# Tile 6 finished between the halves of tile 7's right product, and the gates of tiles 2 to 5 computed in pairs

## The chip, the cores and the metric

The kernel runs on one core of a Trainium2 chip. The metric is the device time of one launch in microseconds (us). The core's engines are TensorE (PE, matrix products), VectorE (DVE), ScalarE (ACT), GpSimd (POOL) and SyncE (SP, which here only issues transfers). Each takes its own instructions strictly in the order in which they are written and waits on semaphores for the others.

## The reference, cut to what matters

For eight tiles x(t) of 128 tokens by 512 features, each with its own adapter number:

```
y = x W + (x A[i]) B[i]                      # base product and the tile's low-rank adapter, rank 16
logits = y W_gate^T                          # 8 experts
p = softmax(logits); keep the top 2, divide by their sum  -> route_w
h = y A_e^T for each expert e (8 x 16 columns);  hw = h * route_w
out = x + y W_base^T + b + hw B              # B: 128 x 512
```

The input is float32 throughout, and the top 2 must come out right.

## The kernel before, in words

The weights are folded first: W is multiplied once with the gate, the experts' A and W_base, and the identity is added, so that a tile needs only x times the folded matrix (648 columns), a low-rank correction, and `hw B`. Precision is kept by splitting each operand into a high part in fp32r and the remainder (`hi`, `lo`); `product` (L808) then issues three matmuls. A split is a cast by ScalarE and a subtraction by VectorE (`lo`, L588).

A tile's result lies in two banks of PSUM. The **left** bank holds the logits (8 columns), h (128 columns) and half of the output, the **right** bank the other half. `Left` and `Right` are its products (tiles 0 to 3). Tiles 4 to 7 are computed two at a time, pair q = 2 with tiles 4 and 5 and pair q = 3 with tiles 6 and 7, by Strassen's scheme with seven products instead of eight, `M1` to `M7`: M5, M4, M3 and M2 fill the left banks; M1, M7 and M6 go into the right ones, with sums in between on VectorE (`sum_e`, `sum_z`, `seed_u`, `sum_u1`, `sum_u2`). Pair 2 has its sums written into the bank ahead of M7 and M6 (`seed_u`); pair 3 has them added at the end (L802, L805).

For a pair q of tiles, `T1(q)` transposes x A, ScalarE copies it (`copy_xa_t`), and `Lora_left(q)` and `Lora_right` multiply it with the adapter part. With `Lora_left(q)` the logits of both tiles are complete, and the gate runs on VectorE (`gate(t)`, L729): max of 8, difference to the first (`top_diff`), index, one-hot, then after ScalarE's `exp_top(t)` the weights and `hw`. `T2(t)` transposes hw, ScalarE and VectorE split the result (`split_hw(t)` on each, through one bank, so that tile t+1's T2 waits for tile t's split), and `Delta(t)` multiplies it with `ffn_b` into the left bank and then the right one (for tile 7 right, then left). ScalarE copies the banks to the output tile (`copy_left`, `copy_right`), which frees them for tile t+4 (left) and t+2 (right): M5(3) waits for the third copy_left, M4(3) for the fourth (L865, L873).

Nothing plans the order: it is written out by hand, one list for each engine. TensorE's list is L1028 to L1080, ScalarE's L526 to L583, VectorE's L751 to L805, GpSimd's L393 to L403 (it forms the sums of x and the low-rank parts, and is done at 38 us), and SyncE's ends with the output transfers, tile by tile (L316 to L325). The left half of tile 7 is sent by ScalarE itself (L583). Since the lists are in order, a wait in one holds up all that stands behind it. The splits that stand between the gates in VectorE's and ScalarE's lists (`split_x_outer`, `split_x_inner`, `split_xd`, `split_cs`) serve the products of pairs 2 and 3.

Of the kernel before, what the change touches and what calls it, by code (L numbers as in the profile page):

```python
# [42 lines left out]
def adaln_ffn_kernel(nc, x_t, itok, fold_in, lora, ffn_b, bias, out):  # L43
    ctx = ExitStack()
    with ctx:
# [161 lines left out]
        def left(t):  # L207
            return left_bank[t % 4]
# [118 lines left out]
        def gpsimd_program(pool):  # L327
# [64 lines left out]

            pool.wait_ge(lora_loaded, NT * DMA)  # L393
# [9 lines left out]
            split_la_pair(3)  # L403

        def scalar_program(act):
# [135 lines left out]
            exp_top(2)  # L541
            copy_right(0)
            copy_right(1)
            exp_top(3)
# [3 lines left out]
            split_cs(SUM7, 4)  # L548
            copy_right_a(2)
# [7 lines left out]
            split_cs(SUM6, 1)  # L557
            copy_left(2)
            exp_top(4)
# [3 lines left out]
            exp_top(5)  # L563
# [12 lines left out]
            copy_left(5)  # L576
            copy_right(5)
            split_hw(6)
            split_hw(7)
# [5 lines left out]
        def vector_program(dve):  # L585
# [111 lines left out]
            def sum_u2(q):  # L697
                k = SEVEN.index(q)
                dve.wait_ge(u1_done, k + 1)
                dve.wait_ge(z_done, k + 1)  # L700
                nc.vector.tensor_tensor(mix(q)[:, 2], mix(q)[:, 2], mix(q)[:, 0], ALU.add).then_inc(u2_done, 1)

# [47 lines left out]

            dve.wait_ge(const_ready, 4)  # L751
# [17 lines left out]
            gate(2)  # L769
            gate(3)  # L770
            sum_e(2)
            split_xa(4)
# [8 lines left out]
            gate(4)  # L781
            gate(5)
            split_hw(4)
            seed_u(2)
            split_cs(SUM7, 2)
            sum_e(3)
            split_xa(6)
            split_cs(SUM6, 3)
# [10 lines left out]
            sum_u2(3)  # L799

            dve.wait_ge(zr_done, NT - 1)
# [5 lines left out]
        def tensor_program(pe):  # L807
# [81 lines left out]
            def seven_right(out, q, which, done, seeded):  # L889
# [3 lines left out]
                for c in range(2):  # L893
                    mm = product(out, xd_chunk(x_hi, q, which, c), xd_chunk(x_lo, q, which, c),
                                 cs_hi[:, which, c, :], cs_lo[:, which, c, :], c == 0 and not seeded, False)
# [11 lines left out]
            def M6(q):  # L907
                pe.wait_ge(yr_done, 2 * q)
                seven_right(right(2 * q + 1), q, SUM6, 3, q == SEVEN[0])
# [135 lines left out]
            M4(2)  # L1045
            T2(2)
            M3(2)
            M2(2)
            T2(3)

            Right(2, ALL)
            T1(2)
# [6 lines left out]
            M4(3)  # L1059
            T2(4)  # L1060
            M1(2)
            M3(3)
            M2(3)
            T2(5)

            M7(2)
            T1(3)
            M6(2)
# [4 lines left out]
            Delta(5)  # L1073
            M7(3)
            T2(6)
            M6(3)
            Lora_right(3, (6, 7))
            T2(7)
            Delta(6)
            Delta(7)  # L1080
# [42 lines left out]
```

## Time and profile before

| | us |
|---|---|
| median of 3 runs | 66.23 (65.94 to 67.05) |
| profiled execution, time | 66.37 |
| its span, first to last instruction | 65.2 |
| TensorE busy | 60.0 (92%), 406 matmuls |
| VectorE busy | 49.9 (77%), 155 instructions |
| ScalarE busy | 33.9 (52%), 91 instructions |
| GpSimd busy | 22.9 (35%), 45 instructions |
| last output transfers, issue to landing | 2.2 (SyncE, 128 KB), 2.9 (ScalarE, 128 KB) |

A row of a timeline tells when an instruction (or a run of like ones) started, how long it took, its engine, its line, the operation and shapes, and in brackets how long the engine had been idle before it and who released it. Instructions overlap in the engines' pipelines, so the next may start before the duration of the one ahead is over; what counts for a queue is the spacing of the starts. Helpers have one line for all calls (a product's matmuls are L809 to L811, every subtraction of a split is L589), so an instruction is told by its tiles and its place in the list. The transposes T1 and T2 are L921 and L952, Lora_left is L935, Lora_right L942.

### The profile page before, as it was taken

How to read it: one execution, taken by the hardware profiler on the slowest of the kernel's cores; microseconds unless marked ns; L12 is line 12 of the kernel's file. 1: busy time of each engine (PE TensorE's matmuls, PEld its weight loads, DVE VectorE, ACT ScalarE, POOL GpSimd, SP SyncE). 2: the span in 40 equal slices, each digit the busy share in tenths (PEclk: the TensorE clock that was granted, in tenths of full speed). 3: DMA queues.
4: the chain of work that ended last, by engine and by line, in shares of the span. 5: the costliest groups of instructions: out<-in, count | busy, mean ns of one | idle time of the engine just before them, and what ended most of it. 6: DMA issues, size and time to landing. Idle time of an engine off the chain costs nothing.

```text
span 65.2 us, 1329 instructions
## 1 busy us (share of the span) xinstructions
PE 60.0 (92%) x406; PEld 58.3 (89%) x406; DVE 49.9 (77%) x155; ACT 33.9 (52%) x91; POOL 22.9 (35%) x45
## 2 busy tenths in 40 slices
PE   4989999999999999999999997999999999999900
PEld 4969999999999999999998995999999997999600
DVE  0957999908799999998888568669766699886800
ACT  2753999315799394452170955478084713452310
POOL 1000799899404994994059930000000000000000
PEclk9999999999999999999999999999999999999999
DMA  0799999404994035323233330810008000034072
GB/s 0 223 339 376 381 398 401 154 3 126 358 329 169 6 96 129 67 61 70 57 78 64 67 79 18 293 49 0 0 9 313 10 0 0 0 134 175 13 263 64
DMA packets 5529, 8.75 MB, mean 134 GB/s; under 512 B 1009, under 2 KB 2065, under 8 KB 5522
## 3 DMA queue, kind: packets, MB, share of 16 engines
q1 hardware_dynamic: 4978, 7.88, 37.4%
q0 software_dynamic: 256, 0.52, 2.3%
q10 hardware_dynamic: 288, 0.27, 1.2%
q8 instruction: 3, 0.05, 0.3%
q14 instruction: 4, 0.03, 0.1%
HBM read 5.26 MB, written 2.10 MB: 113 GB/s over the span
## 4 chain that ended last, share of the span: by engine, by line
PE 78%; DVE 7%; DMA 5%; issue 2%; ACT 2%; DVEq 0%; ACTq 0%
PE bank L809 19%; PE bank L811 18%; PE bank L810 18%; PE bank L817 8%; PE bank L819 5%; DMA w_raw<-fold_in 5%; PE bank L983 3%; PE bank L935 2%; DVE cs_lo L589 2%; PE bank L942 1%; PE bank L987 1%; PE bank L952 1%; PE bank L921 1%; DVE top_diff L735 1%; DVE bank L685 1%
## 5 line engine op out<-in xcount | busy, mean ns | idle before, releaser
L809 PE MATMUL bank<-c_hi,x_hi 128*128 128x408 f32 (+1 forms) x40 | 13.6, 339 | 0.5 <-ACT x_raw L516 0.5
L811 PE MATMUL bank<-c_hi,x_lo 128*128 128x408 f32 (+1 forms) x40 | 13.4, 335 | 0.0
L810 PE MATMUL bank<-c_lo,x_hi 128*128 128x408 f32 (+1 forms) x40 | 13.4, 334 | 0.0
L809 PEld LDWEIGHTS bank<-c_hi,x_hi 128*128 128x128 f32 x40 | 7.5, 188 | 0.8 <-issue 0.8
L589 DVE TENSOR_TENSOR x_lo<-x_raw,x_hi 128x512 fp32r<-128x512 f32 (+1 forms) x10 | 8.0, 824 | 0.0
L810 PEld LDWEIGHTS bank<-c_lo,x_hi 128*128 128x128 f32 x40 | 7.5, 188 | 0.0
L811 PEld LDWEIGHTS bank<-c_hi,x_lo 128*128 128x128 f32 x40 | 7.5, 188 | 0.0
L331 POOL DMA_DIRECT2D lora_raw<-lora x8 | 4.4, 554 | 6.5 <-issue 6.3
L496 ACT ACTIVATE top_exp<-top_diff 128x2 f32<-128x2 f32 x8 | 1.6, 204 | 6.8 <-DVE top_diff L735 6.8
L809 PE MATMUL bank<-ffn_b_hi,hw_hi 128*128 128x256 f32 x16 | 4.9, 305 | 0.0
L811 PE MATMUL bank<-ffn_b_hi,hw_lo 128*128 128x256 f32 x16 | 4.5, 282 | 0.0
L810 PE MATMUL bank<-ffn_b_lo,hw_hi 128*128 128x256 f32 x16 | 4.5, 282 | 0.0
L507 ACT COPY w_raw<-bank 128x256 f32<-128x256 f32 x8 | 2.9, 373 | 2.6 <-PE bank L811 2.5
L503 ACT CAST hw_hi<-bank 128x128 fp32r<-128x128 f32 x8 | 2.1, 267 | 3.3 <-PE bank L952 3.3
L809 PE MATMUL bank<-cs_hi,x_hi 128*128 128x256 f32 x12 | 3.7, 310 | 0.0
L411 ACT CAST wt_hi<-w_raw 128x512 fp32r<-128x512 f32 x4 | 2.5, 620 | 2.3 <-DMA w_raw<-fold_in 2.1
L589 DVE TENSOR_TENSOR hw_lo<-bank,hw_hi 128x128 fp32r<-128x128 f32 x8 | 2.3, 288 | 1.7 <-ACT hw_hi L503 1.7
L977 PE MATMUL bank<-const-bfloat16-1.0 128*128 128x128 bf16 x24 | 2.7, 309 | 0.9 <-PEq L1116 0.9
L589 DVE TENSOR_TENSOR wg_lo<-w_raw,wg_hi 128x648 fp32r<-128x648 f32 (+2 forms) x5 | 3.4, 696 | 0.1
L810 PE MATMUL bank<-cs_lo,x_hi 128*128 128x256 f32 x12 | 3.4, 282 | 0.0
L811 PE MATMUL bank<-cs_hi,x_lo 128*128 128x256 f32 x12 | 3.4, 281 | 0.0
L586 DVE MEMSET bw_rows<- 128x2592 f32 x1 | 2.2, 2218 | 1.5 <-PEq L1116 1.5
(140 smaller groups left out, 188.7 us busy)
## 6 DMA issues: line engine op xcount, KB each, us to landing
x_raw<-x_t SPq DMA_DIRECT2D x8, 256.0 KB, 4.2
out<-w_raw SPq DMA_DIRECT2D x7, 256.0 KB, 2.2
w_raw<-fold_in SPq DMA_DIRECT2D x4, 256.0 KB, 4.6
w_raw<-fold_in SPq DMA_DIRECT2D x3, 324.0 KB, 4.6
bw_rows<-bw_hi SPq DMA_DIRECT2D x16, 40.5 KB, 2.1
lora_raw<-lora POOLq DMA_DIRECT2D x8, 64.0 KB, 3.3
bw_rows<-bw_lo SPq DMA_DIRECT2D x8, 40.5 KB, 2.1
ffn_b_raw<-ffn_b SPq DMA_DIRECT2D x1, 256.0 KB, 5.7
```

Of the source, the lines that this page charges most:

```text
L331: pool.dma_start(lora_raw[:, b, :], lora[bass.ds(adapters[b], 1), :, :].rearrange("a p c -> (a p) c")).then_inc(lora_loaded, DMA)
L411: nc.scalar.copy(wt_hi[:, m, :], raw_wt(m)).then_inc(w_hi_done, 1)
L503: nc.scalar.copy(hw_hi[:, t % 2, :], t2_bank[:, 0:P]).then_inc(hw_hi_done, 1)
L507: nc.scalar.copy(y_out[:, t, y_of_left_bank(t)], left(t)[:, in_left_bank(t)]).then_inc(yl_done, 1)
L586: nc.vector.memset(bw_rows[:, 0].bitcast(F32), 0.0).then_inc(even_zeros, 1)
L589: nc.vector.tensor_tensor(out, raw, hi.bitcast(F32), ALU.subtract).then_inc(done, 1)
L809: nc.tensor.matmul(out, a_hi, b_hi, start=first, stop=False, skip_group_check=True)
L810: nc.tensor.matmul(out, a_hi, b_lo, start=False, stop=False, skip_group_check=True)
L811: return nc.tensor.matmul(out, a_lo, b_hi, start=False, stop=last, skip_group_check=True)
L817: nc.tensor.matmul(bank[i][:, cols], w[:, m, rows], wg[:, m, cols], start=False, stop=False, skip_group_check=True)
L819: nc.tensor.matmul(fold_right(i), w[:, m, rows], wg[:, m, LEFT:], start=False, stop=False, skip_group_check=True)
L977: nc.tensor.matmul(bwr_bank[:, 0:P], ones, ones, start=True, stop=True)
```

## The change

TensorE's list: T2(2) goes behind M3(2), T2(3) behind Right(2), T2(4) behind M1(2), T2(5) behind M7(2), T2(6) ahead of M7(3). M6(3) is cut into its two chunks; between them stand the Lora_right of tile 6, T2(7) and Delta(6), and behind the second chunk the Lora_right of tile 7 and Delta(7).

VectorE's list: gates 2 and 3, and gates 4 and 5, become `gate_pair`, which takes each step for both tiles, with one instruction where the shapes allow it (top_diff, one-hot, reciprocal, weights, route) and two where they don't (max, index, hw). Gates 0, 1, 6 and 7 are as they were. split_cs(SUM7) goes ahead of split_xa(4), split_cs(SUM6) ahead of the hw split of tile 4. sum_u2(3) leaves VectorE for GpSimd, where it waits for the gate of tile 7 as well.

ScalarE's list: exp_top(3) goes ahead of copy_right(0), exp_top(4) and (5) ahead of copy_left(2), split_cs(SUM6) to just behind split_cs(SUM7), and copy_left(5) behind split_hw(6).

No matmul is added or left out.

```diff
--- before.py
+++ after.py
@@ -390,6 +390,13 @@
                                         ALU.subtract).then_inc(la_lo_done, 1)
                 pool.wait_ge(la_lo_done, b + 1)
 
+            def sum_u2(q):
+                k = SEVEN.index(q)
+                pool.wait_ge(z_done, k + 1)
+                pool.wait_ge(hw_done, 2 * q + 2)
+                pool.wait_ge(u1_done, k + 1)
+                nc.gpsimd.tensor_tensor(mix(q)[:, 2], mix(q)[:, 2], mix(q)[:, 0], ALU.add).then_inc(u2_done, 1)
+
             pool.wait_ge(lora_loaded, NT * DMA)
             split_la(0)
             split_la(1)
@@ -401,6 +408,7 @@
             split_la_pair(2)
             sum_x_inner(3)
             split_la_pair(3)
+            sum_u2(3)
 
         def scalar_program(act):
             act.dma_start(w_raw[:, 0, FIRST:D + GH], fold_in[0, :, FIRST:D + GH]).then_inc(w_first_loaded, DMA)
@@ -539,13 +547,14 @@
             copy_left(0)
             copy_left(1)
             exp_top(2)
+            exp_top(3)
             copy_right(0)
             copy_right(1)
-            exp_top(3)
             copy_m5(2)
             copy_m4(2)
             split_hw(2)
             split_cs(SUM7, 4)
+            split_cs(SUM6, 1)
             copy_right_a(2)
             split_hw(3)
             act.wait_ge(x_loaded[6], DMA)
@@ -554,13 +563,12 @@
             split_x_inner(3)
 
             copy_xa_t(2)
-            split_cs(SUM6, 1)
+            exp_top(4)
+            exp_top(5)
             copy_left(2)
-            exp_top(4)
             copy_right(2)
             copy_left(3)
             copy_right(3)
-            exp_top(5)
             copy_m5(3)
             copy_m4(3)
             split_hw(4)
@@ -573,9 +581,9 @@
             copy_left(4)
             copy_right(4)
             exp_top(7)
-            copy_left(5)
             copy_right(5)
             split_hw(6)
+            copy_left(5)
             split_hw(7)
             copy_left(6)
             copy_left(7)
@@ -694,12 +702,6 @@
                 dve.wait_ge(m1_done, k + 1)
                 nc.vector.tensor_tensor(mix(q)[:, 0], first_bank[:, M1_COLS], mix(q)[:, 0], ALU.add).then_inc(u1_done, 1)
 
-            def sum_u2(q):
-                k = SEVEN.index(q)
-                dve.wait_ge(u1_done, k + 1)
-                dve.wait_ge(z_done, k + 1)
-                nc.vector.tensor_tensor(mix(q)[:, 2], mix(q)[:, 2], mix(q)[:, 0], ALU.add).then_inc(u2_done, 1)
-
             steps = [0]
 
             def step(instruction):
@@ -748,6 +750,34 @@
                                                scalar=top_rcp[:, n], in1=route[:, n].unsqueeze(2).broadcast_to([P, E, R]),
                                                op0=ALU.mult, op1=ALU.mult).then_inc(hw_done, 1)
 
+            def gate_pair(q):
+
+                pair = (2 * q, 2 * q + 1)
+                dve.wait_ge(lg_done, q + 1)
+                for t in pair:
+                    top = nc.vector.max(top_val[:, t % 2], left(t)[:, gate_cols(t)])
+                step(top)
+                nc.vector.tensor_tensor(top_diff[:], top_val[:, :, 0:TOP], top_val[:, :, 0:1].broadcast_to([P, 2, TOP]),
+                                        ALU.subtract).then_inc(diff_done, 2)
+                for t in pair:
+                    top = nc.vector.max_index(top_idx[:, t % 2], top_val[:, t % 2], left(t)[:, gate_cols(t)])
+                step(top)
+                step(nc.vector.tensor_tensor(onehot[:], expert_id[:].unsqueeze(1).unsqueeze(1).broadcast_to([P, 2, TOP, E]),
+                                             top_idx[:, :, 0:TOP].unsqueeze(3).broadcast_to([P, 2, TOP, E]), ALU.is_equal))
+                dve.wait_ge(exp_done, pair[1] + 1)
+                nc.vector.reciprocal(top_rcp[:], top_sum[:])
+                step(nc.vector.tensor_tensor(weighted[:], onehot[:],
+                                             top_exp[:].unsqueeze(3).broadcast_to([P, 2, TOP, E]), ALU.mult))
+                step(nc.vector.tensor_tensor(route[:], weighted[:, :, 0, :], weighted[:, :, 1, :], ALU.add))
+                for t in pair:
+                    n = t % 2
+                    if t >= 2:
+                        dve.wait_ge(t2_done, t - 1)
+                    h = left(t)[:, h_cols(t)].rearrange("p (e r) -> p e r", e=E)
+                    nc.vector.scalar_tensor_tensor(out=hw[:, n].rearrange("p (e r) -> p e r", e=E), in0=h,
+                                                   scalar=top_rcp[:, n], in1=route[:, n].unsqueeze(2).broadcast_to([P, E, R]),
+                                                   op0=ALU.mult, op1=ALU.mult).then_inc(hw_done, 1)
+
             dve.wait_ge(const_ready, 4)
             split_xa(0)
             split_xa(1)
@@ -766,9 +796,9 @@
             split_hw(1)
             split_cs(SUM1, 1)
 
-            gate(2)
-            gate(3)
+            gate_pair(1)
             sum_e(2)
+            split_cs(SUM7, 2)
             split_xa(4)
             split_hw(2)
             split_xa(5)
@@ -778,14 +808,12 @@
             split_x_inner(3)
             split_xd(2)
 
-            gate(4)
-            gate(5)
+            gate_pair(2)
+            split_cs(SUM6, 3)
             split_hw(4)
             seed_u(2)
-            split_cs(SUM7, 2)
             sum_e(3)
             split_xa(6)
-            split_cs(SUM6, 3)
             split_xa(7)
             split_hw(5)
             sum_z(3)
@@ -796,8 +824,8 @@
             split_hw(6)
             sum_u1(3)
             split_hw(7)
-            sum_u2(3)
-
+
+            dve.wait_ge(u1_done, len(SEVEN))
             dve.wait_ge(zr_done, NT - 1)
             nc.vector.tensor_tensor(y_out[:, NT - 2, 0:HALF], right(NT - 2), mix(3)[:, 0], ALU.add).then_inc(last_right_done, 1)
             dve.wait_ge(u2_done, len(SEVEN))
@@ -886,11 +914,11 @@
                 pe.wait_ge(m4_copied, SEVEN.index(q) + 1)
                 seven_left(2 * q + 1, 0, C01, q, False).then_inc(left_done, 1)
 
-            def seven_right(out, q, which, done, seeded):
+            def seven_right(out, q, which, done, seeded, chunks=(0, 1)):
                 pe.wait_ge(xd_lo_done, SEVEN.index(q) + 1)
                 if q == SEVEN[0]:
                     pe.wait_ge(cs_lo_done, done)
-                for c in range(2):
+                for c in chunks:
                     mm = product(out, xd_chunk(x_hi, q, which, c), xd_chunk(x_lo, q, which, c),
                                  cs_hi[:, which, c, :], cs_lo[:, which, c, :], c == 0 and not seeded, False)
                 return mm
@@ -904,9 +932,9 @@
                 pe.wait_ge(yr_done, 2 * q - 1)
                 seven_right(right(2 * q), q, SUM7, 2, q == SEVEN[0])
 
-            def M6(q):
+            def M6(q, chunks):
                 pe.wait_ge(yr_done, 2 * q)
-                seven_right(right(2 * q + 1), q, SUM6, 3, q == SEVEN[0])
+                seven_right(right(2 * q + 1), q, SUM6, 3, q == SEVEN[0], chunks)
 
             def T1(q):
                 pe.wait_ge(xa_done, 2 * q + 2)
@@ -1043,12 +1071,12 @@
             Lora_left(1)
             M5(2)
             M4(2)
+            M3(2)
             T2(2)
-            M3(2)
             M2(2)
+
+            Right(2, ALL)
             T2(3)
-
-            Right(2, ALL)
             T1(2)
             Right(3, ALL)
             Lora_left(2)
@@ -1057,26 +1085,28 @@
             Delta(3)
             M5(3)
             M4(3)
+            M1(2)
             T2(4)
-            M1(2)
             M3(3)
             M2(3)
+
+            M7(2)
             T2(5)
-
-            M7(2)
             T1(3)
-            M6(2)
+            M6(2, (0, 1))
             Lora_left(3)
             Lora_right(2, (4, 5))
             Delta(4)
             M1(3)
             Delta(5)
+            T2(6)
             M7(3)
-            T2(6)
-            M6(3)
-            Lora_right(3, (6, 7))
+            M6(3, (0,))
+            Lora_right(3, (6,))
             T2(7)
             Delta(6)
+            M6(3, (1,))
+            Lora_right(3, (7,))
             Delta(7)
 
         sync_program(nc.sync)
```

## Rows read from the trace of the kernel before

**Rows 1.** Windows view: stretch, length, busy us (instructions) per engine, clock, DMA, GB/s.

```profile
36.00:66.00 30.00, 25.19 (x176) 24.11 (x174) 20.06 (x86) 13.47 (x48) 2.07 (x6) 1.00 0.24 80
```

**Rows 2.** TensorE timeline: start us, duration us, engine, line, operation [idle before <- releaser].

```profile
39.66 0.35 PE L811 MATMUL bank<-c_hi,x_lo 128*128 128x408 f32 x1
39.84 0.27 PE L952 MATMUL bank<-ident,hw 128*128 128x128 f32 x1
40.59 0.43 PE L809 MATMUL bank<-c_hi,x_hi 128*128 128x408 f32 x1 [0.47 <-ACT x_raw L516]
```

**Rows 3.** ScalarE timeline around exp_top(2), the right copies, exp_top(3), copy of M5.

```profile
38.29 0.20 ACT L496 ACTIVATE top_exp<-top_diff 128x2 f32<-128x2 f32 x1 [0.79 <-DVE top_diff L735]
...
38.49 0.62 ACT L511 COPY w_raw<-bank 128x256 f32<-128x256 f32 x2
39.89 0.20 ACT L496 ACTIVATE top_exp<-top_diff 128x2 f32<-128x2 f32 x1 [0.77 <-DVE top_diff L735]
...
40.09 0.35 ACT L516 COPY x_raw<-bank 128x256 f32<-128x256 f32 x1
```

**Rows 4.** VectorE timeline: tile 2's gate, then tile 3's top_diff.

```profile
38.02 0.23 DVE L735 TENSOR_SCALAR top_diff<-top_val 128x2 f32<-128x2 f32 x1
...
38.69 0.16 DVE L741 RECIPROCAL top_rcp<-top_sum 128x1 f32<-128x1 f32 x1
38.77 0.16 DVE L742 TENSOR_TENSOR weighted<-onehot,top_exp 128x16 f32<-128x16 f32 x1
...
39.63 0.23 DVE L735 TENSOR_SCALAR top_diff<-top_val 128x2 f32<-128x2 f32 x1
```

**Rows 5.** TensorE timeline: T2(3), T1(2), Lora_left(2), M5(3).

```profile
42.90 0.27 PE L952 MATMUL bank<-ident,hw 128*128 128x128 f32 x1
...
44.43 0.27 PE L921 MATMUL bank<-ident,xa_rows 128*114 128x128 f32 x1
...
45.96 0.52 PE L935 MATMUL bank<-bw_rows,xa_t 114*128 114x392 f32 x2
...
47.99 0.35 PE L809 MATMUL bank<-c_hi,x_hi 128*128 128x408 f32 x1
```

**Rows 6.** VectorE timeline: hw split of tile 3, sum_z(2), wide splits, gate(4).

```profile
43.51 0.29 DVE L589 TENSOR_TENSOR hw_lo<-bank,hw_hi 128x128 fp32r<-128x128 f32 x1
43.72 0.41 DVE L672 TENSOR_TENSOR x_raw<-x_raw,bank 128x256 f32<-128x256 f32 x1
44.04 2.16 DVE L589 TENSOR_TENSOR x_lo<-x_raw,x_hi 128x512 fp32r<-128x512 f32 x3
46.52 0.17 DVE L734 MAX8 top_val<-bank 128x8 f32<-128x8 f32 x1 [0.32 <-PE bank L935]
```

**Rows 7.** ScalarE timeline: hw split of tile 3, copy of T1(2), copy_left(2).

```profile
43.21 0.27 ACT L503 CAST hw_hi<-bank 128x128 fp32r<-128x128 f32 x1 [0.42 <-PE bank L952]
...
44.73 0.27 ACT L492 CAST xa_t<-bank 114x128 fp32r<-114x128 f32 x1 [0.22 <-PE bank L921]
...
47.11 0.37 ACT L507 COPY w_raw<-bank 128x256 f32<-128x256 f32 x1 [1.59 <-PE bank L811]
```

**Rows 8.** TensorE and VectorE timelines: T2(5), Lora_left(3); split_xd(3).

```profile
53.28 0.27 PE L952 MATMUL bank<-ident,hw 128*128 128x128 f32 x1
...
55.28 0.52 PE L935 MATMUL bank<-bw_rows,xa_t 114*128 114x392 f32 x2
...
54.80 0.95 DVE L589 TENSOR_TENSOR x_lo<-x_raw,x_hi 128x768 fp32r<-128x768 f32 x1
```

**Rows 9.** TensorE and ScalarE timelines: last matmul of Delta(6), first of Delta(7), last copy.

```profile
60.57 0.28 PE L811 MATMUL bank<-ffn_b_hi,hw_lo 128*128 128x256 f32 x1
60.82 0.39 PE L809 MATMUL bank<-ffn_b_hi,hw_hi 128*128 128x256 f32 x1
...
61.84 0.37 ACT L507 COPY w_raw<-bank 128x256 f32<-128x256 f32 x1 [0.93 <-PE bank L811]
```

**Rows 10.** GpSimd timeline: the sum of 512 columns, nearest to the sum moved there.

```profile
23.12 1.30 POOL L370 TENSOR_TENSOR x_raw<-x_raw 128x512 f32<-128x512 f32 x1
```

## The prediction

> **What bounds the kernel now.** First the busy time by engine over the second half. From 36 us to the end of the instructions TensorE (PE) is busy 25.2 of 30.0 us, and the last 3.5 us of these hold only the last copy and its transfer; its granted clock is 1.00 [rows 1]. So the set work of TensorE is the spine, and a change that adds and removes no matmul can move the end only through the gaps between matmuls and through what stands behind the last one. The timeline then shows these gaps. The large one is at M3(2): the transpose before it starts at 39.84, the first matmul of M3(2) at 40.59 with 0.47 us idle before it, released by the copy of M5 on ScalarE [rows 2]. That copy (40.09) stood in ScalarE's queue behind exp_top(3), which started at 39.89 [rows 3], because its input, tile 3's top_diff, was written only at 39.63, 1.61 us after tile 2's, by the serial gates on VectorE [rows 4]. The two others are small. From T2(5) at 53.28 to Lora_left(3) at 55.28 [rows 8] lie twelve matmuls (1.43 by the spacing worked out below) and two transposes (0.2), which leaves 0.3: T1(3) waits there for VectorE. And Delta(7) starts at 60.82, 0.25 behind its neighbour instead of 0.12 [rows 9]. With 0.7 for the first (below) the gaps are worth about 1.1 us, which is the most that this change can give.
>
> **Part 1: gates of tiles 2 and 3 as a pair, both exps ahead of the right copies.** The pair has one top_diff write for both tiles. What precedes it is one max more. The trace shows unwaited neighbours on VectorE 0.08 us apart (38.69 to 38.77), and waited ones about 0.20 (the eight steps of a gate take 1.61, 38.02 to 39.63) [rows 4]; the second max is unwaited, so I take 0.08 and keep 0.20 as the upper end. Top_diff of both then starts at 38.10 instead of 38.02 and 39.63. ScalarE followed top_diff by 0.27 (38.02 to 38.29) and an exp held it 0.20 [rows 3, 4]: exps at 38.37 and 38.57, the two right copies (0.62 together) from 38.77, the copy of M5 at 39.39 instead of 40.09. A copy started 0.50 before the matmul that waits for it (40.09 to 40.59) [rows 2, 3], so M3(2) can start at 39.89. TensorE reaches it at 39.84, since T2(2) now stands behind it. Gain at M3(2): 0.7 us. T2(2) used to lie in the stall and now costs its own time. Its price alone isn't in the rows; between 0.06 (by its 128 columns, from the spacings 0.12 for 256 [rows 9] and 0.18 for 408 [rows 2]) and 0.27, I take 0.1. Net: TensorE is 0.6 us ahead from M2(2) on. If the second max took 0.20, it would be 0.5.
>
> A page's rule speaks against the pair. The rows show the 0.08 us between two unwaited instructions [rows 4]. The Trainium skill, VectorE: DVE Perf Modes, section The DRAIN you can't avoid, says that the pipeline empties after every operation and that leaving out the semaphore between operations saves nothing. By that rule the second max, find and scaling would cost full steps, the pair's top_diff would be 0.12 us later twice, and the sum below would come out 0.1 to 0.2 us higher; the row decides, and I stay with 0.08.
>
> **Part 2: T2(3) behind Right(2).** This is where I expect the gain to be given back. Before, T2(3) started at 42.90; twelve matmuls of Right(2) lie between it and T1(2) at 44.43, so they take 1.43 us, 0.119 each [rows 5]. After, T2(3) starts at 42.90 - 0.6 + 1.43 = 43.73, 0.83 later than before although TensorE is ahead. ScalarE split tile 3's hw at 43.21, 0.31 behind the transpose, VectorE at 43.51, another 0.30 [rows 5 to 7]. So VectorE's split_hw(3) comes at 44.34, and queued behind it on VectorE are sum_z(2) and three splits of 512 and more columns (2.16 us together): from 43.51 to 46.20 now [rows 6], 2.69 us, hence to 47.03 after. VectorE had only 0.32 us idle ahead of gate(4) at 46.52 [rows 6], so 0.83 of delay comes through as 0.5: the pair of tiles 4 and 5 starts at 47.03. On ScalarE the two splits of x and the copy of T1(2)'s result stand behind split_hw(3) as well. They ended 0.22 before T1(2) let the copy go at 44.73 [rows 7]; 0.83 later they put that copy at 45.3, and Lora_left(2), which TensorE would reach at 45.96 - 0.6 = 45.36 [rows 5], starts at about 45.6 (0.27 of copy and 0.05 behind it). That takes 0.2 of the gain. VectorE's split_cs(SUM7), moved ahead of split_xa(4), waits for ScalarE's split of the same tile behind split_hw(2) at about 42.1 and runs 0.6 us; split_xa(5) is then done at about 43.7, just when T1(2) wants it. I cost it at nothing; the cover has no slack, so the upper end is 0.3. In its old place it stood 0.6 us ahead of split_xa(6) and (7), as SUM6's did, and T1(3) waited for these: its gap of 0.3 goes.
>
> **Part 3: exps of tiles 4 and 5 ahead of copy_left(2).** Before, copy_left(2) started at 47.11, ahead of exp_top(4) [rows 7], and M5(3) at 47.99 without a wait [rows 5]. M5(3) overwrites the bank that this copy empties. Now the copy stands behind both exps, and they behind the pair's top_diff: 47.03 + 0.21 + 0.08 = 47.32 for top_diff (0.21 is one waited step), exps at 47.6 and 47.8, the copy at 48.0, M5(3) at 48.5 by the 0.50 above. TensorE gets there at 45.6 + (47.99 - 45.96) = 47.63 [rows 5]. New stall: 0.9 us. M5(3) is at 48.5 against 47.99: TensorE has gone from 0.6 ahead to 0.5 behind. M4(3) finds its bank empty: copy_left(3) follows by 0.5, M4(3) by 1.1. This term hangs on VectorE's 0.83 of delay: were the pair there at 46.1, when Lora_left(2) ends, the copy would stand at 47.1 and the stall would be nil. Between those ends (0 and 0.9, 1.1 with slow pair steps) I take 0.9, since each link has its row.
>
> **Part 4: T2(5) behind M7(2).** T2(5) was at 53.28 [rows 8]; after it is at 53.28 + 0.5 + 6 x 0.119 = 54.5. ScalarE +0.31, VectorE +0.30, sum_z(3) +0.21 (43.51 to 43.72) [rows 6]: 55.35. Lora_left(3) waits for sum_z(3), which takes 0.41: 55.35 + 0.41 + 0.1 = 55.85, against 55.28 before. TensorE alone would be there at 55.28 + 0.5 - 0.3 = 55.5: a wait of 0.35. VectorE goes on with split_xd(3) (0.95 [rows 8]) from 55.7 and starts gate(6) at 56.65.
>
> **Part 5: the end.** Gates 6 and 7 stay serial, 1.61 us each [rows 4]: done at 59.85. Then split_hw(6), 0.29 and 0.05 behind it: T2(7) at 60.2 (it needs that bank free). TensorE would be there at 59.9: from Lora_left(3) two matmuls at 0.18, thirty at 0.119 and T2(6), 4.0 us. That is 0.3 of wait. Behind it come Delta(6) (6 matmuls), the second half of M6 (3) and one Lora_right (1): 10 x 0.119 + 0.1 = 1.3, and a restart after a wait costs some 0.07. Delta(7) starts at 61.55. It was at 60.82 [rows 9]: +0.73, with the 0.13 in it that the new order wins by hiding tile 7's hw split, so that Delta(7) no longer waits. Last copy 61.84 + 0.7 = 62.5 [rows 9], the transfer behind it as before. Sum_u2(3) on GpSimd: 256 columns took VectorE 0.41, and the nearest GpSimd row is 1.30 for 512 columns [rows 10], so 0.65 to 1.30. It starts at about 60.6 (behind sum_u1(3) and gate 7) and is done at 61.9 at worst; VectorE's last add needs it at 62.2. Hidden, worth nothing; VectorE loses 0.33 of work where it waits for TensorE anyway. Output transfers on SyncE keep their order; tile 6's leaves more ahead of the last ones, which can give 0 to 0.3 (I take 0).
>
> **Sum**, against the profiled execution (66.37 us, span 65.2): -0.7 (M3) + 0.1 (T2) + 0.2 (Lora_left(2)) + 0.9 (M5(3)) - 0.3 (T1(3)) + 0.35 (Lora_left(3)) + 0.3 (T2(7)) - 0.13 (Delta(7)) = +0.7, so 67.07. That execution stands 0.14 above the median of the three runs (66.23), so the median to expect is 66.95.
>
> **Rivals.**
> (a) Forecast, new waits at Lora_left(2), M5(3) and Lora_left(3): +0.7 (own range +0.3 to +1.2), chance 0.75. For it: each link is an in-order queue with a row, and the 0.32 us of slack on VectorE is smaller than the 0.83 of delay.
> (b) Not slower: the pair of tiles 4 and 5 comes in time, as VectorE makes up for the late T2(3) or its wide splits run faster behind a late start. Then M5(3) starts at 47.6 and the end comes 0.2 earlier than now (66.0); with sum_z(3) in time as well, 0.7 to 0.8 earlier (65.45). It decides from the point where VectorE is free at 46.2 instead of 47.03. Chance 0.18. Against it: nothing on VectorE between split_hw(3) and the pair is taken out.
> (c) Slower by over 2%: the clock. TensorE now idles 0.9 us at M5(3), longer than in any gap named above. In the rows the granted clock stays 1.00 across the 0.47 us gap [rows 1, 2]; no row shows it at the lower level here. If it fell to half after 48.5, each 0.7 us of matmuls would cost 0.7 more, and with one such stretch the time is 67.65. Chance 0.05.
> (d) The change doesn't do what it says: the copy of M5 still comes late (ScalarE waits for the second exp), so the first gain is missing: +1.2 to +1.4, 67.5. Chance 0.02, as both exps need just one top_diff.
>
> **The numbers.** Point 66.95, from (a). Two per cent, about what a measurement of this kernel can tell from no change, is 1.32 us: 64.9 and 67.55. The three runs shown spread by 1.1 us, so a median carries 0.2 to 0.3 of its own. Faster by over 2% needs (b) whole and a low median: 0.03. Slower by over 2%: (c), (d) and the upper end of (a): 0.09. Within: 0.88. Range 66.15 to 67.6: it leaves out most of (b) and some of the upper ends, about 2 in 10.
>
> **What would show it.** In the changed kernel's timeline: no idle ahead of M3(2) (right: start near 39.9); T2(3) near 43.7, VectorE's next gate near 47.0; TensorE idle ahead of M5(3) by 0.8 to 0.9 us, released by a copy to the output on ScalarE; a short wait at Lora_left(3) for the subtraction on VectorE; no idle ahead of Delta(7). Wrong would be: M5(3) without a wait, or the granted clock below 1.00, or the last transfer released by VectorE's add.

## The result, and the profile after

The change makes the kernel about 1% faster: median 65.68 us against 66.41 in 21 runs each, ratio 0.990 (95% interval 0.987 to 0.9925), so 0.7 us. I had forecast 66.95, 0.7 us slower than the 66.23 I knew, with a range from 66.15. The sign is wrong, and that the size is the same is chance: the trace says in which part I was wrong. The ratio compares the fast executions of both kernels alone; each kernel has some that take about 1 us longer, and they count in the medians.

The profiled executions themselves differ in a part that the change doesn't touch. That of the changed kernel took 66.56 us, more than the 66.37 before. Up to M4(2) both lists of TensorE are the same; Lora_left(1), two products ahead of that point, starts at 37.25 us before and at 38.11 after, and between 36.75 and 38.11 in the profiled executions of all kernels below. So I count stages from it (times "from Lora_left(1)"), and let only the timed runs say what a kernel is worth as a whole.

TensorE's timeline of the changed kernel, from the Lora_left of pair 1 on: Lora_left(1) itself, the first matmul of M3(2), T2(3), Lora_left(2), M5(3), T2(5), Lora_left(3), T2(7), tile 7's Lora_right, and Delta(7).

```profile
38.11 0.52 PE L963 MATMUL bank<-bw_rows,xa_t 114*128 114x392 f32 x2
...
40.71 0.35 PE L837 MATMUL bank<-c_hi,x_hi 128*128 128x408 f32 x1
...
44.46 0.27 PE L980 MATMUL bank<-ident,hw 128*128 128x128 f32 x1
...
46.30 0.64 PE L963 MATMUL bank<-bw_rows,xa_t 114*128 114x392 f32 x2
...
49.11 0.42 PE L837 MATMUL bank<-c_hi,x_hi 128*128 128x408 f32 x1 [0.51 <-ACT w_raw L515]
...
55.19 0.27 PE L980 MATMUL bank<-ident,hw 128*128 128x128 f32 x1
...
56.56 0.59 PE L963 MATMUL bank<-bw_rows,xa_t 114*128 114x392 f32 x2 [0.28 <-DVE x_raw L680]
...
60.83 0.30 PE L980 MATMUL bank<-ident,hw 128*128 128x128 f32 x1
...
62.03 0.28 PE L970 MATMUL bank<-bw_rows,xa_t 114*128 114x256 f32 x1
62.15 0.28 PE L837 MATMUL bank<-ffn_b_hi,hw_hi 128*128 128x256 f32 x1
```

The last two rows show Delta(7) start 0.12 us behind the matmul ahead of it, without a wait, where it waited before [rows 9]. The idle ahead of M3(2) [rows 2] is gone. In its place stand the two waits that I had named, at M5(3) for a copy to the output on ScalarE and at Lora_left(3) for the subtraction `sum_z(3)` on VectorE (L680).

VectorE and ScalarE in the same kernel, the rows that answer to [rows 6] and [rows 7]: the hw split of tile 3, sum_z(2), the three wide splits and the gate pair of tiles 4 and 5; on ScalarE that tile's cast, the two exps and copy_left(2).

```profile
45.07 0.29 DVE L597 TENSOR_TENSOR hw_lo<-bank,hw_hi 128x128 fp32r<-128x128 f32 x1 [0.62 <-ACT hw_hi L511]
45.28 0.41 DVE L680 TENSOR_TENSOR x_raw<-x_raw,bank 128x256 f32<-128x256 f32 x1
45.61 2.16 DVE L597 TENSOR_TENSOR x_lo<-x_raw,x_hi 128x512 fp32r<-128x512 f32 x3
47.68 0.24 DVE L758 MAX8 top_val<-bank 128x8 f32<-128x8 f32 x2
48.03 0.16 DVE L760 TENSOR_TENSOR top_diff<-top_val 128x4 f32<-128x4 f32 x1
```

```profile
44.77 0.27 ACT L511 CAST hw_hi<-bank 128x128 fp32r<-128x128 f32 x1 [0.42 <-PE bank L980]
...
48.23 0.20 ACT L504 ACTIVATE top_exp<-top_diff 128x2 f32<-128x2 f32 x1 [1.98 <-DVE top_diff L760]
...
48.43 0.19 ACT L504 ACTIVATE top_exp<-top_diff 128x2 f32<-128x2 f32 x1
...
48.62 0.35 ACT L515 COPY w_raw<-bank 128x256 f32<-128x256 f32 x1
```

VectorE's wide splits end at 47.77 and the gate pair starts without idle, so ScalarE stands idle for 1.98 us ahead of the exp, with copy_left(2) behind it, whose matmuls were done at 47.5.

| from Lora_left(1), us | before | forecast | after |
|---|---|---|---|
| M3(2) | 3.34 | 2.64 | 2.60 |
| T2(3) | 5.65 | 6.48 | 6.35 |
| Lora_left(2) | 8.71 | 8.35 | 8.19 |
| M5(3) | 10.74 | 11.25 | 11.00 |
| Lora_left(3) | 18.03 | 18.60 | 18.45 |
| Delta(7) | 23.57 | 24.30 | 24.04 |
| last copy on ScalarE | 24.59 | 25.25 | 24.95 |
| end of span behind the last copy's start | 3.34 | as before | 2.31 |

Up to the last copy the changed kernel is 0.36 us **slower**. It wins 1.03 us behind it, where I had put 0 (0.3 at most). The two make -0.67, which is what the timed runs give. The 0.36 is no accident of one trace: two more kernels with the changed kernel's body, padded ones below, have their last copy at 24.94 and 25.01, and one with the body of before, the one without tile 6's transfer, has it at 24.55. The view of transfers shows where the rest lies: first rows for the changed kernel from 63 us to its end (mean busy share of the 16 transfer engines in tenths, GB/s, and by issue the size and the time to landing), and then for the kernel before from 63 us to its end (the q14 row gives packets, MB and share of a queue).

```profile
DMA  0000549998998997415999999999997300000000
GB/s 0 0 0 0 205 171 444 444 410 307 375 444 307 410 410 273 137 51 171 307 358 375 358 358 325 342 342 324 358 358 239 120 17 0 0 0 0 0 0 0
...
out<-w_raw ACTq DMA_DIRECT2D x1, 128.0 KB, 1.9
```

```profile
GB/s 373 335 317 466 354 372 317 280 280 373 372 317 354 317 168 75 19 0 19 0 37 19 19 37 19 19 19 37 19 19 19 0 0 0 0 0 0 0 0 0
...
q14 instruction: 1, 0.01, 0.9%
```

Each number of a GB/s line is one fortieth of the window, here 0.055 to 0.06 us. In the changed kernel the last bytes flow at 307 to 375 GB/s until they run out. Before, they flow at 280 to 466 GB/s for 0.8 us and then at 0 to 37, some 20 in the mean, for another 0.8 us: about a sixteenth of the rate, as if one of the 16 transfer engines were finishing its share alone. The same view from 63.93 to 64.73 us, the slow rest by itself, has the two output queues and nothing else:

```profile
DMA packets 17, 0.02 MB, mean 19 GB/s; under 512 B 2, under 2 KB 17, under 8 KB 17
...
q10 hardware_dynamic: 9, 0.01, 2.9%
q1 hardware_dynamic: 8, 0.01, 2.8%
```

The packets' times in the trace, which the view only sums up, have these 17 one behind the other, with 5 ns of overlap at most: seven of 1 KB of SyncE's transfer (q1), then eight of 1 KB of ScalarE's (q10), each group followed by one packet of 4 bytes, and most of them 0.042 us apart. From 63 us on there is one packet of a kind that the changed kernel's end doesn't have: 8 KB (0.01 MB) on the instruction queue q14, from 63.20 to 63.51. The page of the kernel before counts four such fetches in the span, that of the changed kernel three.

```profile
q14 instruction: 4, 0.03, 0.1%
```

```profile
q14 instruction: 3, 0.02, 0.1%
```

Whether the order of the transfers or the fetch did it is what the experiments had to show.

### The profile page after: what moved, and what is told of

It reads as the page before. It is cut to its first block, busy times and chain, and to the rows that moved or that the text cites. A ratio compares the mean times of both kernels' runs of the same rounds, so it can differ in the third digit from the quotient of the medians.

```text
span 65.4 us, 1319 instructions
## 1 busy us (share of the span) xinstructions
PE 60.8 (93%) x406; PEld 59.0 (90%) x406; DVE 47.4 (72%) x144; ACT 33.8 (52%) x91; POOL 22.6 (34%) x46
## 4 chain that ended last, share of the span: by engine, by line
PE 82%; DVE 6%; DMA 5%; ACT 3%; issue 1%; DVEq 0%
PE bank L837 20%; PE bank L839 19%; PE bank L838 19%; PE bank L845 8%; PE bank L847 5%; DMA w_raw<-fold_in 5%; PE bank L1011 3%; DVE x_lo L597 3%; PE bank L963 2%; PE bank L980 2%; PE bank L1015 2%; PE bank L970 1%; DVE x_raw L680 1%; ACT w_raw L515 1%; DVE hw_lo L597 1%
## 5 line engine op out<-in xcount | busy, mean ns | idle before, releaser
L398 POOL TENSOR_TENSOR x_raw<-x_raw 128x256 f32<-128x256 f32 x1 | 0.7, 739 | 22.2 <-DVE x_raw L703 22.2
```

## The experiments

**The end alone, and all but the end.** My first theory (T) was that tile 6's 256 KB, now sent earlier relative to the last halves, no longer crowd them. The rival (B) was that the body gains.

```diff
 # the kernel before, with (lines of the list joined)
-            M7(3); T2(6); M6(3); Lora_right(3, (6, 7)); T2(7); Delta(6); Delta(7)
+            T2(6); M7(3); M6(3, (0,)); Lora_right(3, (6,)); T2(7); Delta(6); M6(3, (1,)); Lora_right(3, (7,)); Delta(7)
 # sum_u2(3) from VectorE to GpSimd, copy_left(5) behind split_hw(6)
```

> The kernel before with the end of the change alone: M6(3) in two halves with tile 6 finished between them, T2(6) ahead of M7(3), copy_left(5) behind split_hw(6), sum_u2(3) on GpSimd. Gates and the transposes of tiles 2 to 5 stay as before. Theory T (the gain lies in the transfers at the end: tile 6's 256 KB leave earlier relative to the last two halves of tile 7, so the last one lands in 1.9 us and not 2.9): 0.9 to 1.2 us faster than before, more than the whole change, with the last copy at most 0.2 earlier. Theory B (the gain lies in the body, the end is worth what my prediction gave it): 0 to 0.3 us faster.

Measured: ratio 0.998 (0.993 to 1.003), no difference; last copy 24.45 from Lora_left(1), 0.14 earlier than before, and ScalarE's transfer took 2.9 us again. T's 0.9 to 1.2 us isn't there; B's 0 to 0.3 isn't excluded (the interval is 0.5 faster to 0.2 slower).

```profile
DMA  0000004999999726999999971001001000000000
...
q14 instruction: 1, 0.01, 0.5%
...
out<-w_raw ACTq DMA_DIRECT2D x1, 128.0 KB, 2.9
```

Here tile 6's transfer is clearly apart from the last two (the dip to 2 in the line of the window 62 us to the end), and the slow rest is there all the same, with the instruction fetch (64.15 us).

```diff
 # the changed kernel, with the end put back as it was before
```

> The changed kernel with the end put back: M7(3), T2(6), M6(3) whole, Lora_right of both tiles, T2(7), Delta(6), Delta(7); copy_left(5) ahead of copy_right(5); sum_u2(3) on VectorE. Gates in pairs and the later transposes stay. Theory T: slower than before by 0.2 to 0.5 us, since M5(3) and Lora_left(3) wait (Lora_left(1) to last copy 0.3 to 0.5 longer) and the last transfer lands in 2.9 us as before. Theory B: faster by 0.4 to 0.7 us.

Measured: ratio 0.996 (0.992 to 1.000). The last copy comes at 25.05, 0.46 later than before, so by T this kernel should have been slower. It isn't (0.3 us faster, between 0 and 0.5), since its transfer landed in 2.0 us although the order of the last transfers is that of before, and there is no q14 row:

```profile
out<-w_raw SPq DMA_DIRECT2D x1, 256.0 KB, 2.0
out<-w_raw SPq DMA_DIRECT2D x1, 128.0 KB, 1.9
out<-w_raw ACTq DMA_DIRECT2D x1, 128.0 KB, 2.0
```

Theory T falls with these two, and B with them, since the body of this kernel is the slower one. The long landing comes with the fetch, and the fetch at the end is missing where the gates are in pairs.

A small part is left for T. In the three kernels with the old end and no fetch in it (this one, the padded kernel before and the one with the first pair alone) ScalarE's transfer lands in 2.04 us, and in the five with the new end and no fetch in it in 1.87 or 1.88. So of the 1.03 us behind the last copy, about 0.87 goes with the fetch and 0.16 with the new order.

**The last transfers with less beside them.**

```diff
 # the kernel before, with (the waits beside it left out)
-            for t in range(NT - 1):        # output transfers of SyncE
+            for t in range(NT - 2):
```

> The kernel before without the output transfer of tile 6 (its rows of the output are not written, and nothing waits for them); all computation is as before. Theory T: the two last transfers have the queues to themselves, the one issued by ScalarE lands in about 2.0 us instead of 2.9, and the time is 0.8 to 1.0 us less. Theory B: at most 0.2 us less.

Measured: ratio 0.990 (0.985 to 0.995), 0.7 us, between what T and B named; landing 2.4 us, fetch at the end present. With half the bytes in the queues the transfer still took longer than the 1.9 us of the changed kernel, which sends them all. By the packets, fifteen of the sixteen shares were through 1.49 us behind the issue (1.69 before), and the late one 0.42 behind them (0.79 before). So this kernel mixes less crowding, 0.2 us, with a milder meeting of fetch and output, and prices neither alone.

**The fetch, moved without touching any work.** Theory F: VectorE's program is read in blocks of 8 KB, and before the change a block boundary is reached while the last output is on its way; the paired gates shorten the program (the trace has 191 instructions of VectorE before, waits counted, and 178 after; 190 with the end alone, 179 without the end), and the boundary is no longer reached. If so, instructions that do nothing should be able to bring the gain and to take it away. `even_zeros` is a semaphore raised at about 3.7 us, so that waiting for it costs only the instruction; two waits share one, as 32 of them make 207 out of 191.

```diff
 # the kernel before, with VectorE's list at its start and ahead of gate(2)
+            for _ in range(16):
+                dve.wait_ge(even_zeros, 1)
```

> The kernel before with 16 waits for a raised semaphore at the start of VectorE's list and 16 ahead of gate(2), both where VectorE is idle: its program becomes longer, so that the boundary at which the last fetch falls is passed well before the end. Theory F: the fetch comes before 62 us, ScalarE's transfer lands in about 2.0 us, and the time is 0.5 to 1.0 us less than before, with no work taken out. Theory T, or a gain by fewer instructions as such: the same or slower by up to 0.3 us.

Measured: ratio 0.9905 (0.985 to 0.996), so as much as the change gained, with 16 instructions more and nothing taken out. The last copy came 0.11 later (24.70; 0.09 of it is there at M3(2), behind the waits ahead of gate(2)), the transfer landed in 2.0 us, and the fetch starts at 58.95 us, in the window from 58.5 to 59.5:

```profile
q14 instruction: 1, 0.01, 2.1%
```

and in the last 1.9 us (from 62 us on) there is none:

```profile
GB/s 172 474 345 345 517 302 388 259 517 259 474 259 474 302 345 345 324 345 366 366 366 302 324 345 324 345 345 345 345 281 173 65 0 0 0 0 0 0 0 0
...
out<-w_raw ACTq DMA_DIRECT2D x1, 128.0 KB, 2.0
```

The same waits in the kernel with the end alone price the new end with the fetch out of the way:

```diff
 # the kernel with the end alone, with the same 32 waits
```

> The kernel with the end of the change alone (tile 6 between the halves of tile 7's right product, sum_u2(3) on GpSimd), with the same 32 waits as in the padded kernel before. Against that kernel it prices the new end by itself with the fetch out of the way. Theory F: 0.1 to 0.2 us faster than the padded kernel before (0.7 to 1.1 faster than before). Theory T: 0.9 to 1.1 faster than the padded kernel before.

Measured: ratio 0.989 (0.983 to 0.996), against 0.9905 for the padded kernel before: the timed runs tell no difference. But this pair doesn't price the new end cleanly, since the moved fetch brings a pause on VectorE. Its row and that of T2(7) on TensorE:

```profile
58.27 0.16 DVE L745 RECIPROCAL top_rcp<-top_sum 128x1 f32<-128x1 f32 x1 [0.45 <-DVE onehot L742]
...
59.44 0.30 PE L958 MATMUL bank<-ident,hw 128*128 128x128 f32 x1 [0.36 <-DVE hw_lo L597]
```

From one-hot to reciprocal in gate 7 VectorE takes 0.62 us here and in the padded kernel before, and 0.25 in the kernel before. The late instruction is the 192nd of VectorE's trace in both padded kernels, and the fetch follows it by 0.65 to 0.67 us; the kernel before has only 191. So a block boundary seems to hold VectorE up as well, though only these two traces show it. The old end hides the pause; the new one needs tile 7's hw earlier, T2(7) waits, and the last copy comes at 24.91. Without padding it came at 24.45, 0.14 earlier than before. With the 0.16 of the landing the new end is worth some 0.3 us by the spans, where no pause meets it.

**The reverse, first in the wrong place.**

```diff
 # the changed kernel, behind VectorE's last addition
+            for _ in range(26):
+                dve.wait_ge(e_done, 1)
```

> The changed kernel with 26 waits for a semaphore that was long ago raised, at the very end of VectorE's list, behind its last addition: nothing waits for them, and VectorE's program gets the length that it had before the change. Theory F (the gain of the change is a fetch of 8 KB of instructions that fell into the last output transfers and no longer does, since the paired gates make VectorE's program shorter): an instruction fetch is back in the last 2 us of the trace, ScalarE's output transfer lands in 2.8 to 3.0 us instead of 1.9, and the time is 0.6 to 1.1 us above the changed kernel's (0 to 0.5 slower than before). Theory T (the order of the last transfers): no difference from the changed kernel, 0.7 faster than before.

Measured: ratio 0.990 (0.982 to 0.998), as the changed kernel. The fetch is back, as the window from 64.0 to the end at 64.4 shows, but it starts at 64.2, when the output's packets are through:

```profile
GB/s 0 0 0 0 0 0 0 0 0 0 0 0 0 0 0 0 0 0 0 819 0 0 0 0 0 0 0 0 0 0 0 0 0 0 0 0 0 0 0 0
DMA packets 1, 0.01 MB, mean 20 GB/s; under 512 B 0, under 2 KB 0, under 8 KB 0
...
q14 instruction: 1, 0.01, 8.2%
```

My expectation failed on that: a program of the old length isn't enough, the fetch has to meet the packets. The waits stood behind the last addition and ran until 63.05, and with them the point at which VectorE asks for the block came later. So the same 26 waits ahead of the hw split of tile 4, where VectorE idles for 2.2 us:

```diff
             split_cs(SUM6, 3)
+            for _ in range(26):
+                dve.wait_ge(even_zeros, 1)
             split_hw(4)
```

> The changed kernel with the same 26 waits for a raised semaphore as the kernel padded at its end, but ahead of the hw split of tile 4, where VectorE is idle for 2.2 us. VectorE's program has the old length, and its last instructions stand where they stood in it before the change. Theory F: VectorE's last fetch falls between 0.5 us before and 1.0 us behind the start of ScalarE's output packets, and that transfer lands in 2.4 to 3.0 us instead of 1.9; the time is 0.5 to 1.0 us above the changed kernel's, 0.2 faster to 0.4 slower than before. If the landing of 2.9 in the kernel before has another cause: as the changed kernel, 0.7 faster than before.

Measured: ratio 0.997 (0.993 to 1.001): two thirds of the change's gain gone (0.5 of 0.7 us; the intervals of the two kernels, 0.987 to 0.9925 and 0.993 to 1.001, only just stay apart). The last copy is where the changed kernel has it (24.94 from Lora_left(1), against 24.95), the transfer landed in 2.5 us, and the slow rest is back at 17 to 34 GB/s with the fetch in the window (63 us to the end):

```profile
GB/s 478 375 341 410 307 375 137 103 120 239 478 324 375 341 325 273 376 358 324 307 290 154 34 0 17 17 34 17 34 17 17 34 0 0 0 0 0 0 0 0
...
q14 instruction: 1, 0.01, 0.9%
...
out<-w_raw ACTq DMA_DIRECT2D x1, 128.0 KB, 2.5
```

**The waits that the change makes.**

```diff
 # the changed kernel, with
             copy_xa_t(2)
-            exp_top(4)
-            exp_top(5)
             copy_left(2)
             copy_right(2)
             copy_left(3)
             copy_right(3)
+            exp_top(4)
+            exp_top(5)
```

> The changed kernel with exp_top(4) and (5) behind the four output copies of tiles 2 and 3 instead of ahead of them. Theory T: the 0.5 us wait of TensorE at M5(3) goes, and the end comes 0.4 to 0.9 us earlier than the changed kernel's (1.1 to 1.6 earlier than before). Theory B, or if the waits behind M5(3) swallow it: as the changed kernel, within 0.1.

Measured: ratio 0.980 (0.972 to 0.988), 0.7 us better than the change. M5(3) starts at 10.35 from Lora_left(1) instead of 11.00 and has no wait, and the last copy at 24.23 instead of 24.95: my step for M5(3) stands, with 0.65 for the order of these six lines.

```diff
 # in addition
-            M7(2)
             T2(5)
+            M7(2)
             T1(3)
```

> The changed kernel with exp_top(4) and (5) behind the output copies of tiles 2 and 3, and T2(5) ahead of M7(2) as it was before. Either theory: the wait at Lora_left(3) for sum_z(3) goes as well, 0.2 to 0.4 us less than with the exps alone moved (1.4 to 1.8 us faster than before, 64.3 to 64.9 us). If the wait at T2(7) takes it, no difference from that kernel.

Measured: ratio 0.971 (0.964 to 0.978). Lora_left(3) comes at 17.30 from Lora_left(1), against 17.72 with the exps alone moved, the last copy at 23.74 against 24.23. By the ratios the two intervals overlap; the stage itself is 0.49 shorter. No wait of a matmul is left behind the start-up: the waits of TensorE in this kernel are

```profile
PE bank L1005 <- PEq L1146: 0.9, 1, 0.9
PE bank L1011 <- DMA w_raw<-fold_in: 0.4, 1, 0.4
```

**The first pair alone.**

```diff
 # the kernel before, with
-            gate(2)
-            gate(3)
+            gate_pair(1)
 # exp_top(3) ahead of copy_right(0), T2(2) behind M3(2)
```

> The kernel before with the gates of tiles 2 and 3 alone as a pair, both exps ahead of the two right copies, and T2(2) behind M3(2); nothing else. My step for M3(2): TensorE's 0.47 us idle ahead of it goes, and from M2(2) to the last copy all comes 0.5 to 0.6 us earlier, since no later transpose is moved and copy_left(2) stays ahead of the exps. The program of VectorE is 6 instructions shorter: if the fetch at the end stays (Theory F leaves that open), the time is 0.6 less than before; if it goes, 1.4 less. Rival: the 0.6 is swallowed at T1(3) and the last copy comes at most 0.2 earlier.

Measured: ratio 0.984 (0.977 to 0.990). M3(2) at 2.65, M5(3) at 10.09 (before 10.74), the last copy at 23.93, 0.66 earlier than before: the whole 0.7 of my first step reaches the end when no later transpose is moved. The landing is 2.0 us and no fetch lies at the end (185 instructions of VectorE in the trace); together 1.5 us by the spans of this stage, 1.1 (0.7 to 1.5) by the ratio.

**A version built of what held.**

```diff
 # the kernel before, with both gate pairs, exp_top(3) ahead of copy_right(0), T2(2) behind M3(2),
 # the exps of tiles 4 and 5 behind the four output copies, and the new end;
 # T2(3) to T2(5) and the splits of the sums where they were
```

> The kernel before with both gate pairs and the new end, but with the transposes of tiles 3, 4 and 5 where they were before the change, the exps of tiles 4 and 5 behind the four output copies and the splits of the sums in their old places. By my steps no new wait at Lora_left(2), M5(3) or Lora_left(3): last copy 0.5 to 0.9 us earlier than before and no fetch in the transfers: 1.3 to 1.9 us faster than before, equal to or up to 0.3 better than the best so far (0.971). If the later transposes are worth something by themselves: 0.2 to 0.5 slower than that one.

Measured: ratio 0.973 (0.966 to 0.980), last copy at 23.77: equal to the best so far by both. Either is 1.8 to 1.9 us faster than the kernel before (each interval is 0.4 to 0.5 us either way), and T2(3) and T2(4) one product later are worth nothing: one of the two versions has them later, the other doesn't, and the last copies are 0.03 apart. Where T2(3) is in its old place M5(3) still comes 0.3 earlier (10.04 against 10.36), but by Lora_left(3) the two are level (17.34 and 17.30).

## Why the prediction was wrong, point by point

**M3(2), Part 1: right.** Forecast 2.64, measured 2.60 from Lora_left(1); the pair's second max cost 0.14 (top_diff stands 0.35 behind the first max, and 0.21 before), between my 0.08 and 0.20. So the row that I followed was half right, and so was the rule of the Trainium skill (VectorE: DVE Perf Modes, The DRAIN you can't avoid) that leaving out the semaphore saves nothing: of wide instructions it holds here, since the two hw instructions take 0.61 and one takes 0.35 (the second adds 0.26; the spacing with a wait was 0.27), and of small ones not (two max take 0.24, one 0.17).

**T2(3), Lora_left(2) and M5(3), Parts 2 and 3: right in kind, 0.25 too dear.** T2(3) came 0.70 later than before and not 0.83, VectorE's chain from the hw split to the gate pair took 2.61 and not 2.69, and Lora_left(2) waited less. The wait at M5(3) is there with the releaser that I named; from the last matmul of Delta(3) at 48.33 to M5(3) at 49.11 TensorE lost 0.66 (0.12 is a spacing), against 0.9.

**Lora_left(3) and T2(7), Parts 4 and 5: right.** Both waits are there, and T1(3)'s gap went: Lora_left(3) is 0.42 late where M5(3) was 0.26, so 0.16 more (forecast 0.06), with a wait of 0.43 ahead of it, where I had 0.35, and T2(7) stands 0.16 late behind the Lora_right ahead of it (forecast 0.3). Delta(7)'s wait went, as said. GpSimd's sum took 0.74 us from 61.18 and was done 0.86 ahead of the last addition (62.78), which waited for TensorE: hidden, as forecast.

```profile
61.18 0.74 POOL L398 TENSOR_TENSOR x_raw<-x_raw 128x256 f32<-128x256 f32 x1 [22.24 <-DVE x_raw L703]
```

**"The transfer behind it as before ... I take 0": the step that failed.** I put the change behind the last copy at nothing and took the 2.9 us of ScalarE's last transfer for a property of the transfer, although SyncE's of the same size took 2.2 in the same table. It was 2.0 us of transfer, and 0.9 in which a fetch of VectorE's instructions held up a part of it. The edit changed the length of VectorE's program by 13 instructions, and I had counted their time on the engine only, not their place in the program. The 0.16 that tile 6's earlier transfer brought lies inside the 0 to 0.3 that I had named for it. With -1.0 instead of 0 in the sum, -0.3 would have come out. Of the rest to the measured -0.7, 0.3 is the body: I had the last copy 0.66 later, and it came 0.36 later, most of it by the steps of Parts 2 and 3. For the same reason the 1.1 us that I called the most that this change could give holds for the body alone: the best version has its last copy 0.85 earlier, and is 1.9 us faster.

**The rivals.** (b) gave the right side for the wrong reason: M5(3) did wait, and the gain that (b) needed came with the exps moved. (c) and (d) didn't happen; the granted clock is 1.00 in the profile after.

**Why the fetch costs more than its own 0.3 us, as far as the packets tell.** Behind the fetch of the kernel before, which ends at 63.51, the next packets of the late share start at 63.60, 63.88 and 64.03 and take 0.29 (2 KB), 0.17 and 0.08 us (1 KB each), where the others of these sizes take 0.09 and 0.05; from there on they are as quick as the others. The fetch's 0.31, the pause of 0.09 behind it and what these three take too long come to 0.75 of the 0.79 us by which the share is late. The same slow packets stand behind the fetch in the other three kernels in which it meets the output. In the kernel before and in the one padded in the middle the fetch starts equally far, 0.2 us, ahead of the transfer's first packets (63.2 and 63.4; 63.6 and 63.85), and yet the one lands in 2.9 us and the other in 2.5. Of the 0.4 between them, 0.17 is the order of the end (the fifteen other shares were through 1.69 and 1.52 us behind the issue), and 0.24 the late share itself (0.79 and 0.55 behind the others), with 18 KB still to send behind the fetch in the one and 14 in the other.

What stays open is why the packets next to a fetch are slow. The records name the queue of a packet and not its engine, so that the fetch shares one engine with the late share is argued from their times, not shown by an experiment.

## What to carry to other kernels

When a span ends with output transfers, compare the last one's time to landing with its neighbours of the same size, and look whether the rate of bytes falls to a sixteenth at the end; if an instruction fetch lies there, a change in the length of one engine's program by a dozen instructions can be worth as much as a stall on the busiest engine, as it was here. A change's gain in such a kernel has to be measured in two parts, up to the last compute instruction and behind it, before its mechanism is credited. And a transpose moved one product later is free only while nothing waits behind its consumers: T2(5) cost 0.5 us at the last copy, since Lora_left(3) waited for what stood behind it on VectorE, and T2(3) and T2(4) cost nothing at the last copy once the exps stood behind the copies.

## What the runs showed of the hardware that I had not expected

- An engine's instructions arrive in the middle of the run, as packets among those of the data: q14 packets of 8 KB at 21, 33, 38 and 63 us in the kernel before, the last one moved to 58.95 by 16 instructions more on VectorE and gone with 13 fewer. Of the other three, the padding moved the one at 33 us too, to 26.5; those at 21 and 38 us stayed within 1 us, so they are probably not VectorE's. The Trainium skill, Advanced Engine Details and Errata, section ISA Cache, gives a cache line of 16 KB, or 256 instructions; the trace agrees for queue q8 (three fetches, 0.05 MB) and differs for q14 (four, 0.03 MB: 8 KB each).
- Such a fetch among the last packets of output held its share of them up by 0.4 to 0.9 us in four kernels, as much as the largest idle time of TensorE in the second half (0.47 before, 0.51 after).
- Instructions that do nothing made the kernel 0.95% faster (0.4 to 1.5%).
